# A graph network kernel: the first table by one product of 136 columns per block, with x fetched during the edge lists

## What is computed

```python
def _L0_gnn_ref(in_feat, edge_ind, edge_len, W_proj, a_src, a_tgt, bias):
    proj_feat = (in_feat @ W_proj).reshape(n_nodes, n_head, d_out)      # 4 heads of 32
    src_score = jnp.sum(proj_feat * a_src, axis=-1)
    tgt_score = jnp.sum(proj_feat * a_tgt, axis=-1)
    edge_score = leaky_relu(src_score[src_ind] + tgt_score[tgt_ind], 0.2)
    edge_score = jnp.exp(edge_score - jnp.max(edge_score))
    neigh_sums = segment_sum(edge_score, tgt_ind, num_segments=n_nodes)
    att_per_edge = edge_score / (neigh_sums[tgt_ind] + 1e-16)
    out_feat = segment_sum(proj_feat[src_ind] * att_per_edge[..., None], tgt_ind, num_segments=n_nodes)
    return out_feat.reshape(n_nodes, -1) + bias

x = _layernorm(x + _L0_gnn_ref(x, edge_index, ...))
x = _layernorm(x + _L1_gnn_ref(x, edge_index, ...))
x = _layernorm(x + _L2_gnn_ref(x, edge_index, ...))
return _layernorm(x + _L3_gnn_ref(x, ..., src, dst, edge_type_4))
```

## Time and profile before

| | us |
|---|---|
| median of 3 runs | 5109.95 (5108.88 to 5111.2) |
| the profiled execution, its own time | 5109.49 |
| its span in the trace | 5107.0 |
| `table0`, from SP's first instruction in it to the first in `edges0` | 79.85 (48.35 to 128.20) |

### The profile page before, as it was taken

One profiled execution on the slowest core, in us unless ns is written; L12 is line 12 of the kernel. 1 busy time (PEld: TensorE's weight loads), 2 busy tenths in 40 slices (PEclk: granted clock), 3 DMA queues, 4 the chain that ended last, 5 costly groups with the idle time before them and its releaser, 6 DMA issues. The chain is left out here.

```text
span 5107.0 us, 61146 instructions
## 1 busy us (share of the span) xinstructions
PE 2516.9 (49%) x15195; PEld 2280.4 (45%) x15195; DVE 2018.1 (40%) x5316; ACT 819.4 (16%) x1866; POOL 3298.4 (65%) x3495
## 2 busy tenths in 40 slices
PE   3455555553444444438999644444544333333331
PEld 3344444443344344338999633333433233333331
DVE  3555555552222322237777522322232222222224
ACT  1122222221000000002222101111111111111112
POOL 0777777775777777741111377777776677777775
PEclk6555555555555555555555555555555565655555
DMA  3333333332233232322322222222222445554443
GB/s 86 80 79 81 82 82 80 79 81 48 54 56 55 55 56 55 55 39 81 85 84 84 66 53 69 66 65 65 65 70 58 113 129 133 133 132 130 130 133 98
DMA packets 382812, 414.09 MB, mean 81 GB/s; under 512 B 111946, under 2 KB 281374, under 8 KB 382606
## 3 DMA queue, kind: packets, MB, share of 16 engines
q0 software_dynamic: 108064, 223.66, 19.9%
q1 hardware_dynamic: 268050, 186.77, 13.5%
q10 hardware_dynamic: 6656, 3.21, 0.2%
HBM read 330.84 MB, written 83.80 MB: 81 GB/s over the span
## 5 line engine op out<-in xcount | busy, mean ns | idle before, releaser
L528 POOL DMA_INDIRECT G<-table,IC x3328 | 3150.4, 947 | 1114.6 <-issue 1057.4
L1318 PE MATMUL PS<-SEL,G 128*128 128x96 f32 x1664 | 384.3, 426 | 534.5 <-DMA G<-table,IC 534.1
L1318 PEld LDWEIGHTS PS<-SEL,G 128*128 128x128 f32 x1664 | 362.5, 330 | 557.4 <-issue 544.0
L2147 PE MATMUL PS<-SEL,G 128*128 128x96 f32 x1664 | 361.6, 406 | 457.7 <-DVE SEL L2187 457.7
L990 PE MATMUL PS<-SEL,GW 128*128 128x96 f32 x1664 | 387.9, 428 | 402.0 <-DVEq L1053 402.0
L2416 DVE TENSOR_TENSOR_SCAN GW<-BIG,GW,PS 128x512 f32<-128x512 bf16 x208 | 266.2, 1280 | 779.7 <-PE PS L2391 770.2
L2147 PEld LDWEIGHTS PS<-SEL,G 128*128 128x128 f32 x1664 | 337.6, 310 | 487.9 <-DVE SEL L2187 487.9
L990 PEld LDWEIGHTS PS<-SEL,GW 128*128 128x128 f32 x1664 | 362.8, 330 | 411.6 <-DVEq L1053 411.6
L2391 PE MATMUL PS<-IDENT,G 128*128 128x128 f32 x832 | 204.6, 427 | 677.5 <-DMA G<-table,IC 677.5
L2391 PEld LDWEIGHTS PS<-IDENT,G 128*128 128x128 f32 x832 | 163.2, 223 | 715.9 <-DMA G<-table,IC 531.1
L1963 POOL TENSOR_TENSOR GW<-BIG,WE 128x392 f32<-128x392 f32 x104 | 89.7, 863 | 512.9 <-ACT WE L1950 471.0
(11 more groups left out here) (302 smaller groups left out, 3510.5 us busy)
## 6 DMA issues: line engine op xcount, KB each, us to landing
running_max<-BIG SPq DMA_DIRECT2D x105, 512.0 KB
G<-table,IC POOLq DMA_INDIRECT x3328, 2.5
ROWS<-edge_places SPq DMA_DIRECT2D x209, 192.0 KB, 3.0
G<-source_in_block SPq DMA_DIRECT2D x105, 256.0 KB, 3.2
BIG<-run_mask SPq DMA_DIRECT2D x104, 256.0 KB, 4.5
table<-BIG SPq DMA_DIRECT2D x49, 256.0 KB, 2.6
BIG<-xT SPq DMA_DIRECT2D x1, 3125.0 KB, 13.1
BIG<-x SPq DMA_DIRECT2D x24, 128.0 KB
```

The source lines that it names most:

```text
L528: pool.indirect_dma_start(out=G[:, b, u, 0:width], out_offset=None, in_=table, in_offset=bass.IndirectOffsetOnAxis(ap=IC[:, b * U + u:b * ...
L1318: last = t.matmul(PS[q][:, 0:W], G[:, b, u, 0:D], SEL[:, q, u, :], start=u == 0, stop=u == U - 1)
L2147: last = t.matmul(PS[q][:, 0:W], G[:, b, u, 0:D], SEL[:, q, u, :], start=u == 0, stop=u == U - 1)
```

## The change

`exact3`, a stage that a flag leaves out in these runs, gets one more wait. The rest is this:

- The loads of `w_proj`, `a_src`, `a_tgt`, `xT` and the zero rows of the parts' table, and the DVE steps that make the 8 score columns, move from `table0` into `edge_lists`. The loads are issued by ACT, which had nothing to do there; `xT` is issued when the three small ones have landed. `xT` goes to `XBUF`, which is its own buffer.
- In `table0` PE takes the blocks of x straight from `XBUF`, with one product of 136 columns per block. ACT does nothing in this stage. All of it is written out without a loop, in 17 chunks of 3 blocks (the last of one), with four PSUM banks and four row buffers in turn.
- DVE copies per chunk 132 columns per block into the row buffer in one instruction and the 8 scores into `ST` in a second. After chunks 4, 8, 12 and 17 it splits the target scores of the 12 (at the end 13) new blocks, and SP stores these parts behind the chunk's rows.

```diff
 def edge_lists():
+                @block.scalar
+                def _(act):
+                    act.dma_start(WS[:, 0:D], w_proj).then_inc(x_in, 16)
+                    act.dma_start(SX[:, 0, 0:D], a_src.to_broadcast([P, D])).then_inc(x_in, 16)
+                    act.dma_start(SX[:, 0, D:2 * D], a_tgt.to_broadcast([P, D])).then_inc(x_in, 16)
+                    act.wait_ge(x_in, 48)
+                    act.dma_start(XBUF[:, 0:N], xT).then_inc(x_in, 16)
+                    act.wait_ge(zeroed, 1)
+                    act.dma_start(T0W[NP:NP + W, :], ZERO[0:W, 0:6].bitcast(BF)).then_inc(x_in, 16)
+                    act.wait_ge(x_in, 80)
...
+                    v.memset(XBUF[:, N:WIDE], 0.0)
+                    v.memset(ZERO[:], 0.0).then_inc(zeroed, 1)
+                    dve.wait_ge(x_in, 48)
+                    v.tensor_tensor(YS[:, 0, 0:D], WS[:, 0:D], SX[:, 0, 0:D], ALU.mult).then_inc(heads, 1)
+                    v.tensor_tensor(YS[:, 0, D:2 * D], WS[:, 0:D], SX[:, 0, D:2 * D], ALU.mult).then_inc(heads, 1)
+                    dve.wait_ge(heads, 2)
+                    v.tensor_reduce(WS[:, D:D + 8], YS[:, 0, 0:2 * D].rearrange("p (h d) -> p h d", d=DH), AXX, ALU.add)
                     dve.wait_ge(rows_in, 64)
 def table0():
+            ROW0 = GF[:, 20 * (D + H):32 * (D + H)].rearrange("p (q u f) -> p q u f", q=4, u=3)
+            chunks = [(c, c * 3, min(NB, c * 3 + 3)) for c in range(-(-NB // 3))]
+            quarters = {3: (0, 12), 7: (12, 24), 11: (24, 36), len(chunks) - 1: (36, NB)}
 @block.sync
-                    with sp.Fori(0, NODE_TURNS) as turn:
-                        for b in range(2):
-                            i, nb, blk, col = half(turn, b)
-                            sp.wait_ge(rows_done, i + 3)
-                            sp.dma_start(rows[:, ds(blk, nb), :], YW[:, 4 * b:4 * b + nb, :]).then_inc(stored[b], 16)
-                    sp.wait_ge(parts_ready, 1)
-                    sp.dma_start(T0W[0:NP].rearrange("(b p) f -> p b f", p=P),
-                                 TPART.rearrange("p b r h -> p b (r h)")).then_inc(parts_out, 16)
+                    for c, b0, b1 in chunks:
+                        sp.wait_ge(rows_done, c + 1)
+                        sp.dma_start(rows[:, b0:b1, :], ROW0[:, c % 4, 0:b1 - b0, :]).then_inc(stored[c % 4], 16)
+                        if c in quarters:
+                            p0, p1 = quarters[c]
+                            n += 1
+                            sp.wait_ge(parts_ready, n)
+                            sp.dma_start(part_rows[:, p0:p1, :],
+                                         TPART[:, p0:p1].rearrange("p b r h -> p b (r h)")).then_inc(parts_out, 16)
 @block.tensor
-                            pe.wait_ge(xT_ready, i + 1)
-                            pe.wait_ge(rows_done, i + 1)
-                            for j in range(nb):
-                                blkT = SA[:, b, j * P:(j + 1) * P]
-                                t.matmul(PS[b][:, j * P:(j + 1) * P], blkT, WS[:, 0:D], start=True, stop=True)
-                                last = t.matmul(PS[2 + b][:, j * 8:(j + 1) * 8], blkT, WS[:, D:D + 8],
-                                                start=True, stop=True)
-                            last.then_inc(pe_done, 1)
+                    for c, b0, b1 in chunks:
+                        if c >= 4:
+                            pe.wait_ge(kept, c - 3)
+                        for blk in range(b0, b1):
+                            at = (blk - b0) * (D + 8)
+                            last = t.matmul(PS[c % 4][:, at:at + D + 8], XBUF[:, blk * P:(blk + 1) * P], WS[:, 0:D + 8],
+                                            start=True, stop=True)
+                        last.then_inc(pe_done, 1)
 @block.vector
-                            dve.wait_ge(pe_done, i + 3)
-                            dve.wait_ge(stored[b], 16 * turn + 16)
-                            v.tensor_copy(YW[:, 4 * b:4 * b + nb, 0:D], proj)
-                            v.tensor_copy(YW[:, 4 * b:4 * b + nb, D:D + H], scores[:, :, 0:H])
-                            v.tensor_copy(ST[:, ds(blk, nb), :], scores).then_inc(rows_done, 1)
+                    for c, b0, b1 in chunks:
+                        both = PS[c % 4][:, 0:(b1 - b0) * (D + 8)].rearrange("p (b f) -> p b f", f=D + 8)
+                        dve.wait_ge(pe_done, c + 1)
+                        if c >= 4:
+                            dve.wait_ge(stored[c % 4], 16 * (c // 4))
+                        v.tensor_copy(ROW0[:, c % 4, 0:b1 - b0, :], both[:, :, 0:D + H]).then_inc(rows_done, 1)
+                        v.tensor_copy(ST[:, b0:b1, :], both[:, :, D:D + 8]).then_inc(kept, 1)
+                        if c in quarters:
+                            p0, p1 = quarters[c]
+                            T, PT, RT = ST[:, p0:p1, H:8], TPART[:, p0:p1], TREST[:, p0:p1]
+                            dve.wait_ge(kept, c + 1)
+                            ch.step(v.tensor_copy(PT[:, :, 0, :], T))
+                            ch.step(v.tensor_tensor(RT, T, PT[:, :, 0, :], ALU.subtract))
+                            ch.step(v.tensor_copy(PT[:, :, 1, :], RT))
+                            ch.step(v.tensor_tensor(RT, RT, PT[:, :, 1, :], ALU.subtract))
+                            ch.step(v.tensor_copy(PT[:, :, 2, :], RT))
+                            dve.sem_inc(parts_ready, 1)
```

More of the change, by code:

```diff
@@ L254, in edge_lists @@
             ipart = SC[:, 0:1]
+            x_in, heads, zeroed = sem("list_x_in"), sem("list_heads"), sem("list_zeroed")
             with nc.Block() as block:
@@ L392, in table0 @@
         def table0():
-            x_in, w_in, zeroed, w_ready = sem("t0_x_in"), sem("t0_w_in"), sem("t0_zeroed"), sem("t0_w_ready")
-            xT_ready, pe_done, rows_done = sem("t0_xT"), sem("t0_pe"), sem("t0_rows")
-            stored = [sem("t0_stored0"), sem("t0_stored1")]
+            pe_done, rows_done, kept = sem("t0_pe"), sem("t0_rows"), sem("t0_kept")
+            stored = [sem(f"t0_stored{q}") for q in range(4)]
             red_in, red_out, chain = sem("t0_red_in"), sem("t0_red_out"), sem("t0_chain")
@@ L398, in table0 @@
             rows = T0.rearrange("(b p) f -> p b f", p=P)
+            part_rows = T0W[0:NP].rearrange("(b p) f -> p b f", p=P)
             TPART = GWF[:, 1200:1200 + NB * 6].bitcast(BF).rearrange("p (b r h) -> p b r h", r=3, h=H)
             TREST = GWF[:, 1600:1600 + NB * H].rearrange("p (b h) -> p b h", h=H)
+            ROW0 = GF[:, 20 * (D + H):32 * (D + H)].rearrange("p (q u f) -> p q u f", q=4, u=3)
+            chunks = [(c, c * 3, min(NB, c * 3 + 3)) for c in range(-(-NB // 3))]
+            quarters = {3: (0, 12), 7: (12, 24), 11: (24, 36), len(chunks) - 1: (36, NB)}
             with nc.Block() as block:
@@ L403, in _ @@
                 def _(sp):
[L404 to L409, removed]
@@ L420, in _ @@
[L420 to L431, removed]
+                    n = 0
@@ L433, in _ @@
+                    sp.wait_ge(parts_out, 64)
+                    for q in range(4):
+                        sp.wait_ge(stored[q], 16 * len(chunks[q::4]))
                 @block.tensor
                 def _(pe):
[L435 to L439, removed]
-                            pe.wait_ge(xT_ready, i + 1)
-                            pe.wait_ge(rows_done, i + 1)
-                            for j in range(nb):
-                                blkT = SA[:, b, j * P:(j + 1) * P]
-                                t.matmul(PS[b][:, j * P:(j + 1) * P], blkT, WS[:, 0:D], start=True, stop=True)
-                                last = t.matmul(PS[2 + b][:, j * 8:(j + 1) * 8], blkT, WS[:, D:D + 8],
-                                                start=True, stop=True)
-                            last.then_inc(pe_done, 1)
+                    for c, b0, b1 in chunks:
[6 more added lines that the diff above has]
+                        last.then_inc(pe_done, 1)
@@ L456, in _ @@
                     ch = Chain(dve, chain)
[L457 to L465, removed]
-                                            YS[:, 0, 0:2 * D].rearrange("p (h d) -> p h d", d=DH), AXX, ALU.add))
@@ L467, in _ @@
-                    dve.sem_inc(w_ready, 1)
-                    with dve.Fori(0, NODE_TURNS) as turn:
-                        for b in range(2):
-                            i, nb, blk, col = half(turn, b)
-                            proj = PS[b][:, 0:nb * P].rearrange("p (b f) -> p b f", f=D)
-                            scores = PS[2 + b][:, 0:nb * 8].rearrange("p (b f) -> p b f", f=8)
-                            dve.wait_ge(pe_done, i + 3)
-                            dve.wait_ge(stored[b], 16 * turn + 16)
-                            v.tensor_copy(YW[:, 4 * b:4 * b + nb, 0:D], proj)
-                            v.tensor_copy(YW[:, 4 * b:4 * b + nb, D:D + H], scores[:, :, 0:H])
-                            v.tensor_copy(ST[:, ds(blk, nb), :], scores).then_inc(rows_done, 1)
@@ L479, in _ @@
```

(8 more changed lines are left out.)

4 lines of the change are left out of this document (removed).

## The result

The changed kernel takes 5076.18 us, median of 4 runs (5075.83 to 5077.0), against 5110.17 for the kernel before: a ratio of 0.9934, with a 95% interval of 0.9921 to 0.9946. It is 34 us faster, where 46.4 were forecast, and it lies above the range. The profiled execution took 5075.83 us with a span of 5074.0.

The account below looks back on a forecast made before the run. PE was taken to bound `table0`'s loop; x's fetch +4.0, then 0.1 + 20.0 + 5.75 + 3.1, started `edges0` 46.9 us earlier; with first gather +0.5, 46.4 less than 5109.49 gave 5063.1 us, range 5057.5 to 5071.

Parts of the forecast that it names:

- The saving passes to the end in full: Whole program: what is saved ahead of `edges0` should reach the end in full; 46.9 us earlier start, 46.4 after first gather.
- The head goes: Start of `table0`: PE has everything it needs at once, so 0.1 us in place of 16.72.
- The fetch of x, +4.0: `edge_lists`: fetching x there delays the lists and the start of `table0` by 4.0 us, bounds 0 and 7.8.
- 4 us of x are free: `edge_lists`: engines idle until about 14 us take 4 us of x's fetch free; 3.8 us remain for the lists to share.
- The rival that gave 0 for the fetch: `edge_lists`: the fetch of x is hidden and costs nothing, whole time 5059.1 us; chance 12%.
- The product: `table0` loop: one 136-column product per block takes 0.454 us at the same clock, 22.2 us for 49 blocks.
- The clock rises: `table0` loop: granted clock rises from 0.50 after some 4 us, PE stops being the bound; chance of no rise 17%.
- The stretch, 20.0 between 17.5 and 22.8: `table0`, first product to last copy of scores: 20.0 us for 42.7; DVE gives 17.5, PE at the old clock 22.8.
- the price of a piece: `table0` stores: each piece of the parts takes a quarter of 12.5 us of full DMA use.
- cost by the DMA, not by the count: Rival on parts' stores: a 12-block piece takes the whole's 12.3 us, whole time 5095; chance 6%.
- The tail, 5.75 + 3.1: End of `table0`: last split and DVE's chain 5.75 us, for 17.3, then 3.1 to the start of `edges0`.
- ACT's table load, +0.5: Start of `edges0`: the table load now comes first there and delays the first gather by 0.5 us.

Follow-up runs that it names:

- best_third: late_defer_ring8 timed a third time, in a job of its own on the first kind of chip: 5055.93 us, ratio 0.9896.
- x_late: Changed kernel with xT issued only when the four list loads have landed: 5069.81 us, ratio 0.9921.
- x_half: Changed kernel with x fetched in two halves, the second only when the list loads have landed: 5080.55 us in one run.
- x_pads: Changed kernel with xT issued only when the padding has landed, so together with the list loads: 5084.9 us in one run.
- all_late: late_defer_ring8 with the small loads also issued behind the list loads and score columns made at the end of `edge_lists`: 6019.93 us, ratio 0.9894.
- late_defer_ring8: Changed kernel with x_late and p_end together, the wait for the parts moved into `edges0`, and eight row buffers: 6029.55 us, ratio 0.9902.
- p_act: Changed kernel with the four pieces of the parts issued by ACT instead of SP: stretch 27.5 us in one run, second kind of chip.
- p_end: Changed kernel with the parts stored by one DMA at the end of `table0` instead of four pieces: 5078.89 us, ratio 0.994.

## Why the prediction was wrong, point by point

- **The saving passes to the end in full: right on the first kind of chip.** 33.3 us at the start of `edges0`, 34.0 in the medians; 53.3 and 53.1 in best_third.
- **The head goes: right.** With the shift of `edge_lists` taken off (9.3 us at its last DMA, 54.50 against 45.23), the first product stands at 48.1, where `table0` began. 16.7 us are saved as said.
- **The fetch of x, +4.0: mis-sized, and above its own upper bound of 7.8.** It cost 9.0 us. The step that failed is "4 us of x are free", with "a little for the padding DMAs". The DMA engines were idle then, but the padding DMAs of 7.98 to 9.76 stand on the chain: until they land, no list load is issued. The lists didn't share anything with x; the padding did. Six of the seven are one packet of 16.9 KB each. The packed trace has the start of every packet (us):

| | x ahead of the lists | the six packets start at | last one ends |
|---|---|---|---|
| x_late | none | 9.89, 10.52, 11.15, 11.78, 12.42, 13.05 | 13.68 |
| x_half | 128 packets of 12.5 KB | 9.90, 11.00, 12.56, 14.59, 16.59, 17.69 | 18.32 |
| changed kernel | 128 packets of 25 KB | 9.90, 11.70, 14.32, 17.27, 19.75, 21.32 | 21.94 |

  Without x they follow one another at once, 0.63 us each, as on a single engine. In the changed kernel one or two packets of x, mostly of 0.93 us, pass between each two of them, eight in all (two where the 4-byte packet that reports the DMA before takes a turn of its own). That makes 8.3 us, and the list loads are 8.2 us late against x_late; in x_half it makes 4.6, and they are 4.6 late. Sharing with the lists wouldn't have been cheaper: in x_pads they paid 7.5. The other 0.9 us are the small loads, which I had put beside the copies at no cost (all_late). The rival that gave 0 for the fetch was true of another place only: behind the list loads it is free.
- The Trainium skill (DMA: Bandwidth & Descriptors, "Queues, rings and completion order") says that each DMA engine takes turns between the queues that have work, at packet granularity. The traces agree, with 17 packets of 512 bytes beside 18 of 25 KB in x_pads. So a single small DMA doesn't stand behind all 3.1 MB, but each packet lets one whole packet of the other queue pass. Six DMAs of two packets each were enough turns to let all of x pass that falls to one engine (128 packets over 16 engines are eight), and so the delay came out in proportion to the bytes of x.
- **The product: right.** The copies of the first chunks follow at 1.36 us (59.15, 60.51), 0.453 us per block at the granted clock of 0.50.
- **The clock rises: right**, after 6 us and not 4. It didn't decide in the changed kernel, since PE was not the bound; in late_defer_ring8, with 17.0 us, it did: at 1.2 GHz the products alone take 22.2.
- **The stretch, 20.0 between 17.5 and 22.8: mis-sized, 28.4.** The failing term is the price of a piece. The runs take it apart:

| row buffers | pieces in between | stretch, us |
|---|---|---|
| 8 | no | 17.0 (17.7 and 17.1 when repeated) |
| 4 | no | 21.0 (20.9) |
| 8 | yes | 21.7, and 5 us more at the tail |
| 4 | yes | 28.4 (26.9) |

  DVE alone was sized right, 17.5 for 17.0, rows too, 10.3 for 10.5 us of use. A ring of four costs 4 us; I had taken the sum of full uses as a bound and not asked when the next store can be issued. The pieces cost 7.4 us (in x_late, x_pads, x_half and p_act, also with pieces and four buffers, the stretch is 27.1 to 27.5). I had priced a piece at a quarter of 12.5, 3.1 us, as time of its own and added to the rows' at their old price. The packets of the packed trace, by size (number, mean of one, sum divided by 16 engines), show another thing:

| | 24-byte packets | 528-byte packets (rows) |
|---|---|---|
| changed kernel, stretch | 4608, 10 ns, 2.9 us | 6057, 58 ns, 22.0 us |
| p_act, stretch | 4608, 13 ns, 3.9 us | 6126, 55 ns, 20.9 us |
| p_end, stretch | none | 5659, 29 ns, 10.3 us |
| changed kernel, the last piece | 1664, 7 ns, 0.75 us | none |

  The three pieces themselves took 1.0 us each in the mean. The rows' packets beside and behind them took twice as long as without pieces, some 11 us more for the same number. It begins when a piece is through: at 66 to 67 us its packets run at 40 GB/s, at 68 to 69 us the rows' packets take 179 ns each.

```profile
66.00:67.00 1.00, 1.00 (x10) 1.00 (x10) 1.00 (x5) 0.00 (x0) 0.00 (x0) 1.00 0.67 40
68.00:69.00 1.00, 1.00 (x9) 0.82 (x8) 0.68 (x4) 0.00 (x0) 0.00 (x0) 1.00 1.17 54
```

  The last piece has nothing behind it, and pays nothing:

```profile
88.00:89.00 1.00, 0.00 (x0) 0.00 (x0) 0.54 (x4) 0.00 (x0) 0.27 (x1) 0.50 0.69 37
89.00:90.00 1.00, 0.00 (x0) 0.00 (x0) 0.73 (x5) 0.00 (x0) 0.10 (x1) 0.50 0.07 3
```

  The one store of all parts in the kernel before does the same to itself. The forecast read "DMA share 0.78 throughout"; that is a mean. With no other store in flight, the first 2614 rows (113 to 115 us) need 1.2 us of use, as cheap as the last piece, and the other 3658 need 11.2:

```profile
114.00:115.00 1.00, 0.00 (x0) 0.00 (x0) 0.47 (x3) 0.00 (x0) 0.37 (x1) 0.50 0.74 38
118.00:119.00 1.00, 0.00 (x0) 0.00 (x0) 0.00 (x0) 0.00 (x0) 0.00 (x0) 0.50 2.34 12
```

  So a burst of 24-byte rows is cheap, and what is written in the microseconds behind it is dear, rows of 528 bytes and of 24 alike. The rival "cost by the DMA, not by the count" isn't it, nor is the count. Which memory or engine is behind on its work was not tried.
- **The tail, 5.75 + 3.1: right**, 9.07, with the last piece landed (91.2) before DVE's last flag (91.6).
- **ACT's table load, +0.5: right.** POOL's first gather is 2.47 us behind the start of `edges0`.
- **The range** was built from bounds of single terms. The true price of both terms lay above their bounds, 1.2 us at x and 5.6 us at the stretch: x, because the padding packets took turns with it; the stretch, because the pieces doubled the time of the rows' packets.

## What to carry to other kernels

When a bulk load is moved into idle DMA time, look for the next small DMAs on the critical chain, not only for the next large one, and count how many large packets its packets let pass: here six packets of 16.9 KB, one behind the other, let eight of 25 KB pass and came 8.3 us later. One wait, placed behind the last DMA that the chain needs, gave 8.2 of the 9.0 us back. Many rows of 24 bytes are best written when nobody waits for what is written behind them: one store that runs on into the next stage beat four pieces in between. And a ring's depth and the DMA engines' use are two bounds; more buffers help only where the second leaves room.

## What the runs showed of the hardware that was not expected

- Two queues took turns by packets, whatever their size: beside x (18 packets of 25 KB in a microsecond) the list loads got 17 packets of 512 bytes through, without it 683 (x_pads).
- In the same run a list load of 448 KB, issued while x was being fetched by another queue, held SP for 7.14 us in its issue, where it is 0.56 alone.
- 1664 stored rows of 24 bytes needed 0.75 us of DMA use with nothing behind them. Three pieces of 1536 took 1.0 us each in the mean, and the packets of the 528-byte rows about them 58 ns in place of 29.
- Of 6272 such rows in one store the first 2614 took 7 to 8 ns each, the others 49 ns in the mean, 115 in the slowest microsecond (the kernel before).
- In the kernel before the granted clock stands at 1.00 in the records for the first 45 us, although the 14 transposes there (38.53, 3.19 us) run at 0.228 us each, the pace of those at 0.50 (16 in 3.7 us).
- On two kinds of chip the same kernel took 5110 and 6083 us, with nearly equal times in the first 100 us.
